# Attention projection of six panels as three f32r products in the last stage, and quantiser scales as bf16 pairs

## The chip, the cores and the metric

The kernel runs on one core of a Trainium2 chip. The core has TensorE (matrix products into PSUM; in the profile PE for the products and PEld for the weight loads that run beside them), VectorE (DVE), ScalarE (ACT), GpSimd (POOL), and SyncE (SP), which issues most of the DMAs. The metric is the device time of one execution in microseconds (us), lower is better.

## What is computed

One layer of a graph network on 1250 nodes with 1024 features and 40000 edges. Cut to what matters here:

```python
xn = layernorm(x)
x = x + gnn(xn, edges) + mix(xn)
x = x + ffn(layernorm(x))

# gnn: attention over incoming edges of each node (4 heads of 64)
p = exp(e - segment_max(e, dst)[dst])
out = segment_sum(p / denom[dst] * xl[src], dst) @ W_up
# mix: linear attention, phi = elu + 1, 16 heads
kv   = einsum('bshd,bshe->bhde', phi(k), v)
attn = einsum('bshd,bhde->bshe', phi(q), kv)
mix  = attn @ Wo + bo
# ffn: every operand is fake-quantised to NVFP4 in blocks of 16
sc8 = e4m3(clip(amax / 6 * global_scale, 0, 448))
q   = sign(x) * nearest_fp4(abs(x) / sc8);  result = q * sc8
```

kv and Wo are multiplied first, into a matrix mix_w of 1024 x 1024. What is left of mix is phi(q) @ mix_w: eight panels of 128 features for each node.

## The kernel before

Nodes come in ten chunks (c = 0 to 9) of 125. `build` runs six stages one after the other; their instructions are ordered by hand, each engine has its own program, and semaphores join them. The change concerns the last two.

**`aggregate`** walks over 81 groups (g) of edges; a group is four pairs (q) of 128 edges. For each group SP loads the edge rows (`load_edges`, line 1649 onwards; the DMA itself is line 92) into one of six slots, once TensorE has finished the group six before. VectorE multiplies the rows of two pairs with their weights (`weigh`, line 1833) and writes the one-hot rows of the four pairs (`one_hot`, line 1839, four slots). ScalarE multiplies the rows of the other two pairs (`scale_rows`, line 1784). GpSimd copies eight further columns into the rows (`extras`, lines 1687 and 1688). TensorE then adds everything up in PSUM (lines 1733 and 1735).

Other work is put between the groups by number:
- The quantiser for the weights of the ffn (`PairQuantiser`): each pair m of weight tiles takes VectorE at g = 6m+1, +3, +4 and +5 (`scaled`, `clip`, `push`, `pull`, `product`, lines 1565 to 1582), ScalarE once, and then TensorE transposes and ScalarE copies (`out_tile`).
- Early panels of phi(q) @ mix_w (`early_projection`, line 1750). `EARLY[c]` says how many of the eight panels of chunk c are done here: 4, 3, 3, 3, 3, 2, 2, 0, 0, 0, in two halves of 512 columns. Each half is a piece: its last product stands at group `ENDS_AT[p]`, ScalarE copies it out of PSUM a group later (`out_piece`, line 1791), GpSimd stores it three groups later (`add_piece`): chunks 0 and 1 by an accumulating DMA into `x_bo` (line 73), the others into DRAM (`part_rows`, line 1698). There is one buffer for pieces; ScalarE's next copy waits until the last piece is stored (`piece_kept`), and TensorE's next piece until the copy is done.

**`finish`** takes chunk after chunk. For chunk c TensorE computes the remaining panels (`mix_part`, line 2081, f32, 8 - EARLY[c] panels in each half) and the gnn part (`gnn_part`, line 2086); this is `projections(c)`. VectorE adds it to x (`residual`, line 2352). ScalarE and VectorE normalise the chunk (`deviation` 2205, `scale_of`, `normalise` 2235), VectorE and ScalarE quantise it (`RowQuantiser`: `scales` 1885 to 1891, `clipped` 1899 and 1900, ScalarE's `size_x` 2214, `rounded` 1911 and 1912, `product` 1917). TensorE transposes it and computes the gates (2132), VectorE forms and quantises the hidden rows with the same lines at 512 columns, TensorE computes the down projection (2145). The three are interleaved: in turn c VectorE does hidden(c-2), residual(c), scale_of(c), clip_h(c-2), clip_x(c), round_h(c-2), round_x(c); TensorE does projections(c), turn_x(c-1), down(c-3), gates(c-1). TensorE may start projections(c) once residual(c-1) is done. Phi for chunk c+2 is loaded by SP into one of two slots of `phi_c` when projections(c) are done (line 2023). `x_bo` gets x, the bias and the early part by three DMAs, the latter two accumulating.

In an f32 product TensorE makes two passes, which the profile shows as two instructions. f32r is a type of 32 bits that takes one. An exact enough product of f32 values is made of three f32r ones: high x high, high x low and low x high, where high is the value as f32r and low what is left. An earlier stage does so already (lines 1064 to 1066).

## Time and profile before

| | us |
|---|---|
| median of 3 runs | 1059.26 |
| lowest and highest | 1058.24, 1063.79 |
| profiled execution, own time | 1058.53 |
| its span in the trace | 1056.8 |

In the profiled execution `aggregate` lasts from about 612 to 816 us and `finish` from there to the end. All times below count from the start of the span. A row of the timeline gives the start, the duration, the engine, the line, the operation with its operands, and in brackets how long the engine was idle before it and what released it. Neighbouring instructions of the same form are merged (x8).

### The profile page before, as it was taken

The numbers are of one execution on the slowest core, as the hardware profiler recorded it, in microseconds if no ns is written. First come the engines' busy times: TensorE is split into PE (matmuls) and PEld (weight loads), VectorE is DVE, ScalarE is ACT, GpSimd is POOL, SyncE is SP. The second block draws the span as 40 slices with busy tenths as digits, with TensorE's granted clock in tenths as the row PEclk, the third lists the DMA queues.
The fourth block names the chain that finished last, engine by engine and source line by source line (L and its number), as shares of the span: only waits on it lengthen the run. The fifth ranks groups of instructions, "written<-read, shape, count | busy, mean of one in ns | idle before, by whom it ended". The sixth has DMA issues, their size and how long they took to land. (4 is left out here: it accounts for less than half of the span.)

```text
span 1056.8 us, 17499 instructions
## 1 busy us (share of the span) xinstructions
PE 959.5 (91%) x5429; PEld 794.3 (75%) x5429; DVE 837.9 (79%) x1395; ACT 648.7 (61%) x1435; POOL 496.7 (47%) x582
## 2 busy tenths in 40 slices
PE   2698879999999999999997779999999879999986
PEld 2676779999999999999997357888898334454443
DVE  5875567888888888888888868998995768887776
ACT  3274446665765766666664568999898335554442
POOL 0211777777777777777771524444444200110000
PEclk9699889999999999999998899999999989999998
DMA  9304588989889898998872689989985364674314
GB/s 246 56 7 110 169 243 259 292 265 280 257 254 294 266 287 284 288 280 282 277 244 91 247 198 332 293 278 310 290 270 192 79 135 122 149 160 112 81 19 79
DMA packets 109977, 221.40 MB, mean 209 GB/s; under 512 B 25883, under 2 KB 58228, under 8 KB 109857
## 3 DMA queue, kind: packets, MB, share of 16 engines
q1 hardware_dynamic: 89053, 159.98, 47.2%
q0 software_dynamic: 20576, 60.08, 23.8%
q8 instruction: 50, 0.82, 0.3%
q10 hardware_dynamic: 260, 0.20, 0.1%
q14 instruction: 38, 0.31, 0.1%
HBM read 156.56 MB, written 62.95 MB: 208 GB/s over the span
## 5 line engine op out<-in xcount | busy, mean ns | idle before, releaser
L1024 POOL DMA_INDIRECT score_gath<-xl_rows,misc x324 | 347.4, 1072 | 101.6 <-issue 92.1
L1064 PE MATMUL score_ps_m<-x_hi,score_w_hi 128*128 128x416 f32 (+1 forms) x576 | 209.4, 363 | 2.1 <-DVE score_w_lo L1217 1.9
L1065 PE MATMUL score_ps_m<-x_lo,score_w_hi 128*128 128x416 f32 (+1 forms) x576 | 204.1, 354 | 0.0
L1066 PE MATMUL score_ps_m<-x_hi,score_w_lo 128*128 128x416 f32 (+1 forms) x576 | 204.1, 354 | 0.0
L1784 ACT ACTIVATE agg_gath<-agg_gath,prob 128x64 f32<-128x64 f32 x648 | 159.2, 353 | 6.7 <-DMA agg_gath<-edge_rows 6.4
L1196 DVE TENSOR_TENSOR score_zb<-score_gath,score_ps_x 128x1024 f32<-128x1024 f32 x81 | 98.8, 1219 | 67.6 <-PE score_ps_x L1047 57.9
L1733 PE MATMUL ps_all<-agg_gath,agg_hot 128*125 128x128 f32 x648 | 128.0, 280 | 9.8 <-DVE agg_hot L1839 6.4
L1735 PE MATMUL ps_all<-agg_gath,agg_hot 128*125 128x136 f32 x648 | 128.9, 281 | 0.0
L1733 PEld LDWEIGHTS ps_all<-agg_gath,agg_hot 128*125 128x125 f32 x648 | 100.5, 189 | 25.8 <-issue 25.2
L2081 PE MATMUL ps_all<-mix_w,phi_c 128*125 128x512 f32 x240 | 108.4, 602 | 5.8 <-DVEq L2355 5.2
L1064 PEld LDWEIGHTS score_ps_m<-x_hi,score_w_hi 128*128 128x128 f32 x576 | 109.7, 190 | 4.2 <-issue 2.6
L1065 PEld LDWEIGHTS score_ps_m<-x_lo,score_w_hi 128*128 128x128 f32 x576 | 110.1, 191 | 1.1
L1066 PEld LDWEIGHTS score_ps_m<-x_hi,score_w_lo 128*128 128x128 f32 x576 | 109.3, 190 | 1.5
L1047 PE MATMUL score_ps_x<-parts,score_mask_t 125*128 x648 | 93.7, 287 | 14.6 <-ACT score_mask_t L1119 14.6
L1047 PEld LDWEIGHTS score_ps_x<-parts,score_mask_t 125*128 125x128 f32 x648 | 90.1, 193 | 17.6 <-issue 17.1
L1203 DVE TENSOR_TENSOR score_zb<-score_zb,misc 128x1024 f32<-128x1024 f32 x81 | 98.8, 1219 | 3.4 <-ACT score_zb L1124 3.4
L1204 DVE TENSOR_REDUCE score_e<-score_zb 128x16 f32<-128x1024 f32 x81 | 98.8, 1220 | 2.8
L1735 PEld LDWEIGHTS ps_all<-agg_gath,agg_hot 128*125 128x125 f32 x648 | 97.2, 190 | 0.0
L1117 ACT ACTIVATE score_mask_t<-local_bc,part_iota 125x512 fp32r<-125x512 bf16 x81 | 58.2, 718 | 56.1 <-DMA local_bc<-local_rows 52.7
L2081 PEld LDWEIGHTS ps_all<-mix_w,phi_c 128*125 128x125 f32 x240 | 45.6, 191 | 62.2 <-issue 55.1
L1124 ACT ACTIVATE score_zb<-score_zb 128x1024 f32<-128x1024 f32 x81 | 85.6, 1057 | 10.4 <-DVE score_zb L1196 10.0
L1687 POOL COPY agg_gath<-prob 128x16 f32<-128x16 f32 x81 | 44.2, 549 | 87.4 <-DMA agg_gath<-edge_rows 74.6
(341 smaller groups left out, 1666.3 us busy)
## 6 DMA issues: line engine op xcount, KB each, us to landing
edge_rows<-score_gath SPq DMA_DIRECT2D x81, 528.0 KB, 3.8
agg_gath<-edge_rows SPq DMA_DIRECT2D x81, 528.0 KB, 5.6
local_bc<-local_rows SPq DMA_DIRECT2D x40, 224.0 KB
score_gath<-xl_rows,misc POOLq DMA_INDIRECT x324, 4.5
phi_c<-phi_rows SPq DMA_DIRECT2D x10, 500.0 KB, 6.1
x_bo<-in_x SPq DMA_DIRECT2D x10, 500.0 KB
x_bo<-in_L_mix_bo POOLq DMA_DIRECT2D x10, 500.0 KB, 7.2
out<-fin_x SPq DMA_DIRECT2D x9, 500.0 KB
```

The costliest lines, as they stand in the source:

```text
L1024: nc.gpsimd.indirect_dma_start(out=gath[:, g % GS, q, :], out_offset=None, in_=xl_rows, in_offset=bass.IndirectOffsetOnAxis(ap=src_idx[:, ...
L1047: m = pe.matmul(ps_x[:, u, q // 2, (q % 2) * HID:(q % 2 + 1) * HID], mask_t[:, u, q * TE:(q + 1) * TE], xr_flat[:, ds(cs[q] * (2 * HID) + ...
L1064: pe.matmul(acc, w_hi[:, i % 2, kk, :], x_hi[:, kk, cols], start=(kk == 0), stop=False)
L1065: pe.matmul(acc, w_hi[:, i % 2, kk, :], x_lo[:, kk, cols], start=False, stop=False)
L1066: mm = pe.matmul(acc, w_lo[:, i % 2, kk, :], x_hi[:, kk, cols], start=False, stop=(kk == KC - 1))
L1196: v.tensor_tensor(zb[:, u, :].rearrange("p (q d) -> p q d", q=GP), gath[:, g % GS, :, 0:HID], ps_x[:, u, :, :].rearrange("p h (q d) -> p ( ...
L1203: own.do(v.tensor_tensor(z, z, att_b[:, :].unsqueeze(1).to_broadcast([P, GP, HID]), ALU.mult))
L1204: own.do(v.tensor_reduce(e16[:, :], zb[:, g % 2, :].rearrange("p (a d) -> p a d", d=DH), AX.X, ALU.add))
L1733: pe.matmul(o_flat[0:C, ds(at[2 * q], HALF)], lhs, gath[:, g % GS, q, 0:HALF], start=False, stop=False, skip_group_check=True)
L1735: m = pe.matmul(o_flat[0:C, ds(at[2 * q + 1], UPPER)], lhs, gath[:, g % GS, q, HALF:XW], start=False, stop=False, skip_group_check=True)
L1784: t = act.activation(part, part, ACT.Copy, scale=k.prob[:, g * GP + q, h:h + 1])
L2081: pe.matmul(ps_y[0:C, half, :], phi_c[:, c % 2, kk, :], mix_w[:, kk, half * 512:half * 512 + 512], start=(kk == EARLY[c]), stop=False)
```

## The change

1. `EARLY` is 2 for all chunks: panels 0 and 1 of every chunk are computed in `aggregate`, which makes 20 pieces of two panels instead of 14 of two to four, a piece every 3.6 groups. The number of early panel products stays at 40, that of late ones at 120. Phi for the early panels comes through a ring of four slots; for chunks 6 to 9 SP waits for a piece before it loads.
2. `mix_part` multiplies panels 2 to 7 as three f32r products each. The high and low parts of mix_w are made by GpSimd in `aggregate` (`split_early`, at groups 8, 18, 28, 38, 48 and 58: a copy and a subtraction of 128 x 1024 each, with a wait between). The low part takes the place of mix_w. Three high parts stay in SBUF; those of panels 5 to 7 are stored to DRAM (`mix_rows`) and loaded back by SP at the start of `finish`, into space that the edge rows held.
3. The high part of phi is a copy by ScalarE (`high_phi`, 128 x 750 a chunk), the low part a subtraction by VectorE (`low_phi`, the same size).
4. Both quantisers write the block scale as two equal bf16 values side by side, and round into bf16 (`pull`, `rounded`), so that the last product (`product`) reads bf16 twice and writes bf16, over blocks of 8 x 2 instead of 16.

```diff
@@ -46,7 +46,9 @@
-EARLY = [4, 3, 3, 3, 3, 2, 2] + [0] * (NC - 7)
+EARLY = [2] * NC
+SPLIT = [2, 3, 4, 5, 6, 7]
+SPLIT_KEPT = 3
@@ -71,6 +73,12 @@
+def split_low(nc, k, n, high):
+    kk = SPLIT[n]
+    nc.gpsimd.tensor_tensor(k.mix_lo[:, kk, :], k.mix_w[:, kk, :], high[:, :].bitcast(F32), ALU.subtract).then_inc(k.s_mix_lo, 1)
@@ -197,6 +207,17 @@
+    gath_bytes = 4 * AGG_SLOTS * GP * XW
+    k.gath_at = nc.sbuf_base - gath_bytes
+    assert 4 * D * (len(SPLIT) - SPLIT_KEPT + 1) <= gath_bytes
+    k.s_mix_lo = ctx.enter_context(nc.semaphore("s_mix_lo"))
+    k.s_mix_hi = ctx.enter_context(nc.semaphore("s_mix_hi"))
+    k.s_mix_kept = ctx.enter_context(nc.semaphore("s_mix_kept"))
+    k.s_mix_back = ctx.enter_context(nc.semaphore("s_mix_back"))
+    k.mix_rows = nc.dram_tensor("mix_rows", (len(SPLIT) - SPLIT_KEPT, P, D), F32, kind="Internal").ap()
+    homes = [k.parts_at, k.parts_at + 4 * D, k.kv_at] + [k.gath_at + 4 * D * n for n in range(len(SPLIT) - SPLIT_KEPT)]
+    k.mix_lo = nc.alloc_sbuf_tensor_at("mix_lo", [P, KC, D], F32R, offset=k.mix_at)
+    k.mix_hi = {kk: nc.alloc_sbuf_tensor_at(f"mix_hi{kk}", [P, D], F32R, offset=at) for kk, at in zip(SPLIT, homes)}
@@ -1551,14 +1583,19 @@
-        t, sc8, inv = self.amax[:, kind, :], self.small[:, 0, :], self.small[:, 1, :]
+        t, inv = self.amax[:, kind, :], self.small[:, 1, :]
+        twos = self.scale_twos().rearrange("p (n t) -> p n t", t=2)
...
-        q.do(v.tensor_tensor(sc8, t, p2, ALU.add))
-        q.do(v.tensor_tensor(sc8, sc8, p2, ALU.subtract))
-        q.do(v.tensor_scalar(t, sc8, 2.0 ** -20, -1.0, ALU.max, ALU.mult))
+        q.do(v.tensor_tensor(inv, t, p2, ALU.add))
+        q.do(v.tensor_tensor(twos, inv.unsqueeze(2).to_broadcast([P, NJ * WB, 2]), p2.unsqueeze(2).to_broadcast([P, NJ * WB, 2]), ALU.subtract))
+        q.do(v.tensor_scalar(t, twos[:, :, 0], 2.0 ** -20, -1.0, ALU.max, ALU.mult))
...
+    def scale_twos(self):
+        return self.small[:, 0, :].bitcast(BF16)
@@ -1575,11 +1612,12 @@
-        self.q.do(self.v.scalar_tensor_tensor(out=self.work, in0=self.coarse, scalar=COARSE, in1=self.work, op0=ALU.max, op1=ALU.subtract))
+        self.q.do(self.v.scalar_tensor_tensor(out=self.coarse, in0=self.coarse, scalar=COARSE, in1=self.work, op0=ALU.max, op1=ALU.subtract))
...
-        return self.v.tensor_tensor(self.blocks(out), self.blocks(self.work), self.wide(0, j), ALU.mult)
+        scale = self.scale_twos()[:, 2 * j * self.nb:2 * (j + 1) * self.nb]
+        return self.v.tensor_tensor(by_twos(out), by_twos(self.coarse), twos_over_blocks(scale, self.nb), ALU.mult)
@@ -1647,6 +1686,9 @@
+                def load_early_phi(c):
+                    sp.dma_start(phi_o[:, c % 4, :, :], k.phi_rows[0:2, :, C * c:C * c + C].rearrange("k p n -> p k n")).then_inc(s_phi_o[c % 4], 16)
@@ -1666,8 +1708,12 @@
-                        for c in range(2, 7):
-                            sp.dma_start(phi_o[:, c - 2, :, :], k.phi_rows[0:3, :, C * c:C * c + C].rearrange("k p n -> p k n")).then_inc(s_phi_o, 16)
+                        for c in range(2, 6):
+                            load_early_phi(c)
+                    for c in range(6, NC):
+                        if g == ENDS_AT[2 * (c - 4) + 1] + 4:
+                            sp.wait_ge(s_piece, 2 * (c - 4) + 2)
+                            load_early_phi(c)
@@ -1697,8 +1743,22 @@
+                def split_early(n):
+                    kk = SPLIT[n]
+                    if n > SPLIT_KEPT:
+                        pool.wait_ge(k.s_mix_kept, 16 * (n - SPLIT_KEPT))
+                    high = k.mix_hi[kk] if n < SPLIT_KEPT else mix_stage
+                    nc.gpsimd.tensor_copy(high[:, :], k.mix_w[:, kk, :]).then_inc(k.s_mix_hi, 1)
+                    pool.wait_ge(k.s_mix_hi, n + 1)
+                    split_low(nc, k, n, high)
+                    if n >= SPLIT_KEPT:
+                        nc.gpsimd.dma_start(k.mix_rows[n - SPLIT_KEPT, :, :], mix_stage[:, :].bitcast(F32)).then_inc(k.s_mix_kept, 16)
...
+                    for n in range(len(SPLIT)):
+                        if g == 8 + 10 * n:
+                            split_early(n)
@@ -1880,15 +1940,20 @@
-        t, sc8, inv = (self.small[0:C, i, 0:nb] for i in (0, 2, 3))
+        t, inv = (self.small[0:C, i, 0:nb] for i in (0, 3))
+        twos = self.scale_twos(nb).rearrange("p (n t) -> p n t", t=2)
...
-        q.do(v.tensor_tensor(sc8, t, p2, ALU.add))
-        q.do(v.tensor_tensor(sc8, sc8, p2, ALU.subtract))
-        q.do(v.tensor_scalar(t, sc8, 2.0 ** -20, -1.0, ALU.max, ALU.mult))
+        q.do(v.tensor_tensor(inv, t, p2, ALU.add))
+        q.do(v.tensor_tensor(twos, inv.unsqueeze(2).to_broadcast([C, nb, 2]), p2.unsqueeze(2).to_broadcast([C, nb, 2]), ALU.subtract))
+        q.do(v.tensor_scalar(t, twos[:, :, 0], 2.0 ** -20, -1.0, ALU.max, ALU.mult))
...
+    def scale_twos(self, nb):
+        return self.small[0:C, 2, :].bitcast(BF16)[:, 0:2 * nb]
@@ -1909,14 +1974,12 @@
-        q.do(v.scalar_tensor_tensor(out=a, in0=b, scalar=COARSE, in1=a, op0=ALU.max, op1=ALU.subtract))
+        q.do(v.scalar_tensor_tensor(out=b, in0=b, scalar=COARSE, in1=a, op0=ALU.max, op1=ALU.subtract))
...
-        return self.v.tensor_tensor(out.rearrange("p (n s) -> p n s", s=16),
-                                    self.work[0:C, 0:width].rearrange("p (n s) -> p n s", s=16),
-                                    self.small[0:C, 2, 0:nb].unsqueeze(2).to_broadcast([C, nb, 16]), ALU.mult)
+        return self.v.tensor_tensor(by_twos(out), by_twos(self.coarse[0:C, 0:width]), twos_over_blocks(self.scale_twos(nb), nb), ALU.mult)
@@ -2016,6 +2083,9 @@
+                for n in range(SPLIT_KEPT, len(SPLIT)):
+                    sp.wait_ge(k.s_mix_kept, 16 * (len(SPLIT) - SPLIT_KEPT))
+                    sp.dma_start(k.mix_hi[SPLIT[n]][:, :].bitcast(F32), k.mix_rows[n - SPLIT_KEPT, :, :]).then_inc(k.s_mix_back, 16)
@@ -2077,9 +2147,18 @@
+                    cols = slice(half * 512, half * 512 + 512)
+                    if half == 0:
+                        pe.wait_ge(s_phi_lo, c + 1)
...
-                        pe.matmul(ps_y[0:C, half, :], phi_c[:, c % 2, kk, :], mix_w[:, kk, half * 512:half * 512 + 512],
-                                  start=(kk == EARLY[c]), stop=False)
+                        if half == 0:
+                            pe.wait_ge(k.s_mix_lo, SPLIT.index(kk) + 1)
+                            if kk in SPLIT[SPLIT_KEPT:]:
+                                pe.wait_ge(k.s_mix_back, 16 * (len(SPLIT) - SPLIT_KEPT))
+                        high, low = phi_hi[:, c % 2, kk, :], phi_lo[:, c % 2, kk, :]
+                        pe.matmul(ps_y[0:C, half, :], high, k.mix_hi[kk][:, cols], start=(kk == EARLY[c]), stop=False)
+                        pe.matmul(ps_y[0:C, half, :], high, k.mix_lo[:, kk, cols], start=False, stop=False)
+                        pe.matmul(ps_y[0:C, half, :], low, k.mix_hi[kk][:, cols], start=False, stop=False)
@@ -2090,9 +2169,8 @@
-                    pe.wait_ge(s_phi[c % 2], 16 * (c // 2 + 1))
+                    mix_part(c, 0)
...
-                    mix_part(c, 0)
@@ -2240,6 +2317,12 @@
+                def high_phi(c):
+                    act.wait_ge(s_phi[c % 2], 16 * (c // 2 + 1))
+                    act.activation(phi_hi[:, c % 2, EARLY[c]:, :], phi_c[:, c % 2, EARLY[c]:, :], ACT.Copy).then_inc(s_phi_hi, 1)
+                high_phi(0)
+                high_phi(1)
@@ -2300,7 +2387,16 @@
+                def low_phi(c):
+                    part = phi_c[:, c % 2, EARLY[c]:, :]
+                    v.wait_ge(s_phi_hi, c + 1)
+                    v.tensor_tensor(phi_lo[:, c % 2, EARLY[c]:, :], part, phi_hi[:, c % 2, EARLY[c]:, :].bitcast(F32),
+                                    ALU.subtract).then_inc(s_phi_lo, 1)
+                low_phi(0)
...
+                low_phi(1)
@@ -2424,6 +2522,8 @@
                     round_h(c - 2)
+                    if c + 2 < NC:
+                        low_phi(c + 2)
                     round_x(c)
```

How the instructions stand before and after, at three places. Line numbers of the changed kernel are its own: 1733 and 1734 are `extras`, 1751 and 81 the split, 75 the accumulating DMA.

GpSimd in `aggregate`, around group 8, before:

```order
L1688 COPY agg_gath<-run_max 128x4x4
L73 DMA x_bo<-agg_piece 125x512
L1687 COPY agg_gath<-prob 128x4x4
L1688 COPY agg_gath<-run_max 128x4x4
L1687 COPY agg_gath<-prob 128x4x4
```

The same place now:

```order
L1734 COPY agg_gath<-run_max 128x4x4
L1751 CAST mix_hi_12248<-mix_w 128x1024
L81 TENSOR_TENSOR mix_lo<-mix_w,mix_hi_12248 128x1024
L75 DMA x_bo<-agg_piece 125x512
L1733 COPY agg_gath<-prob 128x4x4
```

Before, the row of the DMA is that of piece 0, behind group 6. Now piece 0's stands behind group 5, and what is shown is the end of group 8 with the first split and piece 1's add behind it.

VectorE in `finish`, the end of the turn of chunk 7 (L1917 and L1982 are the quantiser's last product; `fin_hq` is the hidden row, `misc` holds the quantised x), before:

```order
L1912 SCALAR_TENSOR_TENSOR prob<-prob 125x512
L1917 TENSOR_TENSOR fin_hq<-prob,fin_hid_small 125x512
L1911 SCALAR_TENSOR_TENSOR score<-parts,score 125x1024
L1912 SCALAR_TENSOR_TENSOR score<-parts,score 125x1024
L1917 TENSOR_TENSOR misc<-score,fin_small 125x1024
```

Now:

```order
L1977 SCALAR_TENSOR_TENSOR prob<-prob 125x512
L1982 TENSOR_TENSOR fin_hq<-prob,fin_hid_small 125x512
L2394 TENSOR_TENSOR fin_phi_lo<-phi_c,fin_phi_hi 128x750
L1976 SCALAR_TENSOR_TENSOR score<-parts,score 125x1024
L1977 SCALAR_TENSOR_TENSOR parts<-parts,score 125x1024
L1982 TENSOR_TENSOR misc<-parts,fin_small 125x1024
```

The subtraction for the chunk after next stands between the quantising of the hidden row and that of x.

TensorE at the start of `finish` (L2076 are the transposes of the gnn rows), before:

```order
L1735 MATMUL ps_all<-agg_gath,agg_hot 125x136
L1641 UNCONDITIONAL_BRANCH
L2069 UNCONDITIONAL_BRANCH
L2081 MATMUL ps_all<-mix_w,phi_c 125x512 x8
L2076 MATMUL ps_all<-ident,prob 128x125 x4
```

Now, where the numbers behind mix_hi name the buffers of the panels, 12248 for panel 2:

```order
L1795 MATMUL ps_all<-agg_gath,agg_hot 125x136
L1680 UNCONDITIONAL_BRANCH
L2139 UNCONDITIONAL_BRANCH
L2159 MATMUL ps_all<-mix_hi_12248,fin_phi_hi 125x512
L2160 MATMUL ps_all<-mix_lo,fin_phi_hi 125x512
L2161 MATMUL ps_all<-mix_hi_12248,fin_phi_lo 125x512
L2159 MATMUL ps_all<-mix_hi_12249,fin_phi_hi 125x512
```

Eight f32 products of chunk 0 have become 36 f32r ones, for panels 2 to 7 in two halves, and those of panels 5 to 7 wait for SP's loads.

## Rows read from the trace of the kernel before

**Rows 1.** Busy time by stretch: length, then busy us of each engine, clock, DMA share, GB/s.

```profile
640.00:766.00 126.00, 122.39 (x931) 106.32 (x930) 116.90 (x159) 120.80 (x462) 59.68 (x116) 1.00 0.93 302
766.00:816.00 50.00, 49.17 (x402) 45.27 (x400) 38.65 (x54) 48.11 (x186) 23.92 (x43) 1.00 0.75 245
```

**Rows 2.** Waits of VectorE and of ScalarE, 640 to 766 us: total, times, longest.

```profile
DVE agg_gath L1833 <- DMA agg_gath<-edge_rows: 4.1, 5, 1.4
...
ACT agg_coarse L1806 <- DVEq L1855: 4.0, 2, 2.8
```

**Rows 3.** Timeline of VectorE, line 2352, chunks 0, 1, 2, 4, 8 and 9.

```profile
828.07 1.22 DVE L2352 SCALAR_TENSOR_TENSOR fin_x<-x_bo,ps_all 125x1024 f32<-125x1024 f32 x1 [0.57 <-PE ps_all L2086]
847.69 1.22 DVE L2352 SCALAR_TENSOR_TENSOR fin_x<-x_bo,ps_all 125x1024 f32<-125x1024 f32 x1 [0.22 <-DVE misc L1917]
870.86 1.22 DVE L2352 SCALAR_TENSOR_TENSOR fin_x<-x_bo,ps_all 125x1024 f32<-125x1024 f32 x1 [0.22 <-DVE fin_hid L2386]
908.57 1.22 DVE L2352 SCALAR_TENSOR_TENSOR fin_x<-x_bo,ps_all 125x1024 f32<-125x1024 f32 x1 [0.25 <-DVE fin_hid L2386]
993.07 1.22 DVE L2352 SCALAR_TENSOR_TENSOR fin_x<-x_bo,ps_all 125x1024 f32<-125x1024 f32 x1 [4.45 <-PE ps_all L2086]
1016.13 1.22 DVE L2352 SCALAR_TENSOR_TENSOR fin_x<-x_bo,ps_all 125x1024 f32<-125x1024 f32 x1 [4.45 <-PE ps_all L2086]
```

**Rows 4.** TensorE: from the chain of waits (bf16, f32), then from the timeline (f32r).

```profile
929.43 3.45 PE ps_all L2132 x16
...
952.52 6.87 PE ps_all L2081 x16
...
162.09 0.35 PE L1064 MATMUL score_ps_m<-x_hi,score_w_hi 128*128 128x418 f32 x1
...
163.61 0.35 PE L1066 MATMUL score_ps_m<-x_hi,score_w_lo 128*128 128x418 f32 x1
```

**Rows 5.** VectorE's instructions by form in `finish`: total, mean ns | idle before.

```profile
L1899 DVE TENSOR_TENSOR score<-kv,fin_small 125x1024 f32<-125x1024 f32 x9 | 11.0, 1224 | 0.3
...
L1899 DVE TENSOR_TENSOR prob<-fin_hid,fin_hid_small 125x512 f32<-125x512 f32 x10 | 6.9, 692 | 1.2
...
L1906 DVE TENSOR_SCALAR prob<-prob 125x512 int16<-125x512 int16 x2 | 0.7, 346 | 0.1
```

**Rows 6.** TensorE in `finish`: the chain, the timeline, and the stretch behind 849 us.

```profile
816.25 7.10 PE ps_all L2081 x16
...
849.04 6.61 PE L2081 MATMUL ps_all<-mix_w,phi_c 128*125 128x512 f32 x10 [4.98 <-DVEq L2355]
...
849.00:853.00 4.00, 3.96 (x5) 1.81 (x6) 2.81 (x12) 1.54 (x3) 0.00 (x0) 0.50 0.55 143
```

**Rows 7.** DMA issues, 585 to 600 and 625 to 680 us: size, median us to landing.

```profile
max_wo<-in_L_mix_Wo SPq DMA_DIRECT2D x4, 512.0 KB, 4.4
...
x_bo<-agg_piece POOLq DMA_DIRECT2D x4, 250.0 KB, 7.1
```

**Rows 8.** GpSimd's instructions by form over the whole trace.

```profile
L501 POOL TENSOR_TENSOR parts<-xr,parts 125x256 fp32r<-125x256 f32 x10 | 7.3, 734 | 47.9 <-ACT parts L651 47.9
...
L463 POOL MEMSET kv<- 128x1024 f32 x1 | 0.9, 942 | 0.0
```

**Rows 9.** Timeline of GpSimd and VectorE in an early stage.

```profile
60.08 0.73 POOL L501 TENSOR_TENSOR parts<-xr,parts 125x256 fp32r<-125x256 f32 x1 [10.53 <-ACT parts L651]
60.15 0.94 DVE L780 SCALAR_TENSOR_TENSOR zsum<-zsum 125x256 f32<-125x256 f32 x1
...
71.22 0.42 DVE L780 SCALAR_TENSOR_TENSOR zsum<-zsum 125x256 f32<-125x256 f32 x1
```

**Rows 10.** Timeline of GpSimd: piece 0's add, and the last of `extras` of group 8.

```profile
632.43 0.83 POOL L73 DMA_DIRECT2D x_bo<-agg_piece  x1 [1.07 <-DMA x_bo<-in_L_mix_bo]
...
639.51 0.66 POOL L1688 COPY agg_gath<-run_max 128x16 f32<-128x16 f32 x1
```

More of the change, by code:

```diff
@@ L1536, with by_twos, twos_over_blocks @@
 COARSE = NEAR_ONE * 2.0 ** 22
+def by_twos(ap):
+    return ap.rearrange("p (n r t) -> p n r t", r=8, t=2)
+def twos_over_blocks(row, nb):
+    return row.rearrange("p (n t) -> p n t", t=2).unsqueeze(2).to_broadcast([row.shape[0], nb, 8, 2])
 class PairQuantiser:
@@ L1620, in aggregate @@
         ps_w = ps_m[:, 1, 0:256].bitcast(BF16).rearrange("p (b f) -> p b f", f=P)
-        phi_of = lambda c: k.phi_c[:, c, :, :] if c < 2 else phi_o[:, c - 2, :, :]
+        phi_of = lambda c: k.phi_c[:, c, :, :] if c < 2 else phi_o[:, c % 4, :, :]
         s_load = k.s_load
@@ L1628, in aggregate @@
         s_agg = sem("s_agg")
-        s_phi_o = sem("s_phi_o")
+        s_phi_o = [sem(f"s_phi_o{i}") for i in range(4)]
         s_step = sem("s_step")
@@ L1996, in finish @@
         s_tail = sem("s_tail")
+        s_phi_hi = sem("s_phi_hi")
+        s_phi_lo = sem("s_phi_lo")
         s_pself = sem("s_pself")
@@ L2411, in _ @@
                 clip_x(0)
+                low_phi(2)
                 round_x(0)
@@ L2417, in _ @@
                 clip_x(1)
+                low_phi(3)
                 round_x(1)
```

21 lines of the change are left out of this document (15 added, 6 removed).

## Prediction

> **What bounds the kernel now.** I read the busy time by stretch first, then the waits of each engine there, then the timeline of the places that the change touches. The page names no engine as the bound of the whole, so each of the two stages touched is read by itself.
>
> The aggregation stage ends at 816 us. In its stretch 640 to 766 us three engines are full at once: TensorE 122.4, ScalarE 120.8 and VectorE 116.9 of 126 us [rows 1]. What VectorE lacks is mostly the gap of some 0.06 us between dependent instructions; it really waits 4.1 us there, and ScalarE 4.0 [rows 2]. So some 4 to 5 us of additional work on VectorE finds room, and what is over that moves the stage. From 766 us on VectorE has 11 us free, ScalarE under 2 [rows 1].
>
> The last stage handles ten chunks of 125 nodes. The start of line 2352 marks each: 828.07, 847.69, 870.86, two later 908.57, and 993.07 and 1016.13 for the last two [rows 3]. From 870.86 to 908.57 the period is 18.86 us, and VectorE itself releases the next. The period of the last is 23.07 us, and VectorE waits 4.45 us in it for TensorE. So the early chunks are bound by VectorE and the late ones, which have eight late panels instead of five, by TensorE. Behind 1016.13 the chain is nearly all VectorE's.
>
> **TensorE's products.** An f32 product of 128x512 is two instructions of 0.43 us (16 in 6.87), 0.859 in all. An f32r product is one. Its pace at 512 columns isn't in the trace: at 418 columns it is 0.190 us (162.09 to 163.61 for 8) [rows 4], which by columns gives 0.233. The lower bound is bf16's pace at 512, 0.216 (16 in 3.45); 0.25 is my upper one. Three cost 0.70 instead of 0.86. There are 120 late panels before and after, only spread evenly (12 products of a chunk instead of 8 to 16), and 40 early ones. What else is in a period is 23.07 - 16 x 0.859 = 9.3, so TensorE's period becomes 9.3 + 12 x 0.70 = 17.7 us. That is less than VectorE's: TensorE stops being the bound, and its gain is capped there.
>
> **VectorE in the last stage.** Each chunk adds one subtraction of 128x750 (low_phi): between 512 elements at 0.692 and 1024 at 1.224 [rows 5] that is 0.94, and 0.03 of gap. The quantiser's last product now reads bf16 and bf16, and no row shows such a one. Bounds for 1024 elements: 1.22, as before, and 0.69, twice the pace; half of that for 512. I take the lower ones, because line 1906, with 16 bits in and out, does 512 elements in 0.346, twice 0.692's pace [rows 5]. The Trainium skill ("VectorE: DVE Perf Modes", the perf-mode tier table) has tensor_tensor in bf16 at two elements a cycle, so by it the sum stays. Saved: 0.53 + 0.27 = 0.80. Scales written twice (64 more elements, then 32) add 0.10. Period: 18.86 + 0.97 - 0.80 + 0.10 = 19.13 us. ScalarE gets a copy of 750 elements a chunk, 0.9 us at about 1.15 ns each; it lies before a wait for VectorE, and low_phi covers a late one.
>
> **The start of the last stage.** Before, TensorE starts its panels at 816.25 and ends them at 823.35 [rows 6]; residual 0 follows 4.7 us later. Now ScalarE copies phi, VectorE ends its node steps and subtracts (to 819.0), and TensorE starts 3 us late. Panels 5 to 7 wait for three loads of 512 KB that SP issues only at 816.3. Such a load lands 4.4 us after its issue [rows 7]; two more behind it take 1.7 each at the 300 GB/s of [rows 1]: all landed at 824. 27 products follow, 6.3 us. TensorE has then stood twice for some 3 us. Behind a wait of 4.98 us at 849.04 its granted clock was 0.50, the lower level (1.2 GHz), for 4 us [rows 6]; I add 2 us for that. Panels end at 832.4: +9.0.
>
> Chunk by chunk: residual 0 at 837.1. Residual 1 (VectorE's interval, 19.62 + 0.97 - 0.53 + 0.13): 857.3. Residual 2 (TensorE's interval, 23.17, less 0.5 of panels): 880.0. Six periods of 19.13: residual 8 at 994.8. The last period has no low_phi, 18.2: residual 9 at 1013.0 instead of 1016.13: -3.1. The tail holds one product of 1024 and three of 512: -1.34, scales +0.13. The last stage yields **-4.3 us** (bounds +2 and -9: loads landed at 829 or 821, clock cost 4 or 0, ends of the product's pace).
>
> **The aggregation stage.** TensorE's work there is unchanged, VectorE saves 12 x 0.53. GpSimd gets six splits at groups 8, 18, ... 58, each a copy and a subtraction of 128x1024. GpSimd's rows: a memset of 128x1024 takes 0.94, a subtraction of 125x256 into f32r 0.73, times four 2.9 [rows 8]. I take 1.1 for the copy, which is nearest to the memset, and 2.7 for the subtraction, since a part of the 0.73 is fixed: 3.8 a split, bounds 3.3 and 5.2.
>
> This isn't free for VectorE. At 60.08 GpSimd subtracts for 0.73 us; VectorE's line 780 starts at 60.15 and takes 0.94, to 0.28 us behind GpSimd's end. The same instruction alone takes 0.42, at 71.22 [rows 9]. So GpSimd's instruction locked VectorE's out for its whole length, all but 0.14 us of start. The Trainium skill ("SBUF — State Buffer", Who interferes with whom) states this: a VectorE instruction with two SBUF inputs and a GpSimd one that reads SBUF exclude each other for the whole instruction. The trace agrees, and the rule speaks against this change; all of VectorE's large instructions in the stage are of that kind or rival it for the same ports.
>
> VectorE loses 6 x (3.8 - 2 x 0.14) = 21 us between groups 8 and 60. It saves 9 x 0.53 = 4.8 there and pays 0.5 for longer scales. Of the net 16.8 its waits take 4.1 to 5. It may run up to four groups ahead of TensorE, so I take 1 more off: **+11**.
>
> Two waits more. Pieces come every 3.6 groups instead of 5.1, and one may overwrite the last only when the add of that has landed, 7.1 us after its issue [rows 7]. Piece 0's add goes out at 632.4 and so lands at 639.5; ScalarE now wants piece 1 at group 6, some 3 us sooner. Piece 1's add stands behind the first split on GpSimd: group 8's extras end at 640.2 [rows 10], the split near 645, the add lands at 652.5, while ScalarE wants to overwrite it at group 10, near 650. Behind both stand the weighted rows that TensorE needs. Of these 3 + 2.5 us the first split's lock hides 3.5: **+2**. Six piece copies more on ScalarE (0.6 each) lie mostly in the stretch that VectorE then binds. SP's four waits for a piece delay one edge load each by 2 to 3 us, within the lead of six slots. The stage: **+13** (bounds +5 and +20).
>
> **Sum.** 1058.5 (the profiled execution's own time; the median of the runs is 0.7 more) + 13 - 4.3 = **1067 us**.
>
> **Rivals.**
> 1. *The lock is absorbed.* If GpSimd's split holds VectorE only where it has time, or runs at twice my pace, VectorE's savings and waits pay for it. It decides below 9 us of lock in all, 1.5 a split. Against it: the exclusion at 60.08 [rows 9] is complete, and VectorE has hardly a gap. For it: four slots of one-hot rows and six of edge rows let it run ahead. Then only ScalarE's 3.6 us are left, half hidden: 1058.5 + 1.8 - 4.3 = 1056, not slower than before.
> 2. *The adds hold ScalarE throughout.* 7.1 us of landing stand against 8.9 us from piece to piece, and splits at groups 48 and 58 delay an add again, with 3 MB more to move in a stage whose DMA engines are 93% busy [rows 1]. It decides when an add lands over 8 us behind its copy. At 3 us each for two or three more pieces: 1075.
> 3. *bf16 pairs run at the old pace,* since the innermost run is two elements and nothing here shows such a shape. Last stage 0.8 x 8 + 1.3 = 7.7 more, aggregation 4.8 more: 1079.
> 4. *TensorE's clock falls in each chunk,* since it now waits some 1.4 us in a period. 4 us at the lower level cost 2, of which the slack takes 1.4; over six chunks at most 4 more: 1071.
>
> **Chances.** Forecast 0.52 (1060 to 1075), rival 1 0.20, rival 2 0.12, rival 3 0.06, rival 4 0.05, other 0.05. A difference of 0.5% (5.3 us) is about what a measurement of this kernel tells from none: faster is below 1054, slower above 1064.6. Rival 1 puts half of its chance below 1054, the forecast 0.20 of its own under 1064.6. Faster 0.13, same 0.33, slower 0.54. The range of 1054 to 1077 leaves out rival 3, the upper end of rival 2 and the lower end of rival 1.
>
> **What would show it.** In the aggregation stage: six places where VectorE's instructions of 0.7 us take over 2 while line 81 runs on GpSimd; 10 us or more of waits of TensorE for VectorE or ScalarE; its last group near 829 instead of 816. A product into the bf16 tile at 0.69. In the last stage: f32r products 0.233 apart, the first residual 21 us behind the stage's start instead of 12, periods of 19.1, no waits of 4.45. The forecast is wrong if the aggregation keeps its length, or if the mix_hi loads land before TensorE needs them.

## The result: 1.5% slower

The changed kernel takes 1074.65 us (median of 4 runs, 1073.58 to 1075.28), the kernel before, on the same chip, 1058.75 (1057.07 to 1063.79). The ratio is 1.0146, with a 95% interval of 1.0119 to 1.0172. The forecast had the direction and its range held the time, but it said +8 us and the change costs +16. The profiled executions have spans of 1056.8 and 1073.3 us; what follows is worked out against these.

**Where the time went.** The first and the last product of the aggregation stage mark its length. Two rows of the product line of each kernel, before and then after (instruction, count, shortest/median/longest in ns, first and last start in us):

```profile
L1733 PE MATMUL ps_all<-agg_gath,agg_hot x648: 272/273/542, 612.7 to 815.2; 128*125 128x128 f32 x162
```

```profile
L1793 PE MATMUL ps_all<-agg_gath,agg_hot x648: 272/273/573, 611.6 to 838.6; 128*125 128x128 f32 x162
```

With the end of the very last product (815.8 and 839.2) the stage is 203.0 us long before and 227.5 after: **+24.5**. The last stage, from there to the end, falls from 241.1 to 234.2: **-6.9**. The stage also starts 1.0 us earlier, which is no effect of the change: over all kernels below, none of which changes the work ahead of it, it starts between 610.5 and 616.2. +24.5 - 6.9 - 1.0 = +16.6; the spans differ by 16.5.

The busy times of the aggregation stage as a whole, first of before and then of after (columns: window, its length, then busy us and instructions of TensorE, its weight loads, VectorE, ScalarE, GpSimd; granted clock; DMA share; GB/s):

```profile
612.70:815.80 203.10, 194.09 (x1472) 170.19 (x1472) 174.85 (x238) 184.44 (x705) 90.13 (x170) 0.99 0.89 280
```

```profile
611.70:839.30 227.60, 201.74 (x1472) 177.05 (x1472) 185.68 (x238) 187.32 (x711) 110.56 (x191) 0.96 0.82 264
```

TensorE executes the same 1472 instructions. It is busy 7.7 us longer, at a mean granted clock of 0.96 instead of 0.99, and idle 25.9 us instead of 9.0: the +24.5 are **16.8 us more of waiting and 7.7 us of lower clock**. The forecast had no term for the second. Whom it waits for, and what ScalarE waits for (engine, line, what ended the wait: us in all, times, longest), 612 to 840 us:

```profile
PE ps_all L1793 <- DVE agg_hot L1899: 10.1, 6, 3.1
PE ps_all L1793 <- POOL agg_gath L1734: 6.6, 3, 4.1
PE ps_all L1793 <- ACT agg_gath L1844: 4.9, 2, 3.5
PE ps_all L1793 <- POOL agg_gath L1733: 2.6, 2, 2.1
...
ACT agg_piece L1851 <- DMA part_rows<-agg_piece: 10.5, 3, 8.0
ACT agg_piece L1851 <- DMA x_bo<-agg_piece: 9.0, 1, 9.0
```

Before, no piece copy of ScalarE waited for a DMA at all. Now four of the 20 do, for 19.5 us together.

**The split.** The first of the two lines of GpSimd is the copy, the second the subtraction:

```profile
L1751 POOL CAST mix_hi<-mix_w x3: 1035/1037/1497, 638.1 to 690.6; 128x1024 fp32r<-128x1024 f32 x3
L81 POOL TENSOR_TENSOR mix_lo<-mix_w,mix_hi x3: 2656/2662/2686, 639.2 to 691.7; 128x1024 fp32r<-128x1024 f32 x3
```

1.04 + 2.66 = 3.7 us each; the forecast had 3.8. VectorE's two instructions beside the split at group 48, by the timeline, GpSimd first:

```profile
752.83 1.04 POOL L1751 CAST agg_mix_stage<-mix_w 128x1024 fp32r<-128x1024 f32 x1
753.96 2.66 POOL L81 TENSOR_TENSOR mix_lo<-mix_w,agg_mix_stage 128x1024 fp32r<-128x1024 f32 x1
...
757.13 0.54 POOL L1744 DMA_DIRECT2D part_rows<-agg_piece  x1
```

```profile
752.84 1.57 DVE L1893 TENSOR_TENSOR agg_gath<-agg_gath,prob 128x512 f32<-128x512 f32 x1
754.33 2.82 DVE L1899 TENSOR_TENSOR agg_hot<-node_iota,dst_local 128x500 f32<-128x500 f32 x1
```

Alone they take 0.69 and 0.67. The first ends 0.5 us behind the copy, the second 0.5 behind the subtraction: 3.0 us are lost. (The Trainium skill's rule in "SBUF — State Buffer", Who interferes with whom, that a VectorE instruction with two SBUF inputs and a GpSimd one that reads SBUF shut each other out for a whole instruction, holds here once more.) An instruction of VectorE with one input was held too: its line 1607, 0.69 us alone, took 1.57 at 638.06, beside the copy of the first split at 638.05. The row at 757.13 is the store of a piece that ScalarE had copied at 748.81: it stood behind the split. ScalarE's next rows:

```profile
748.81 0.58 ACT L1851 ACTIVATE agg_piece<-ps_all 125x512 f32<-125x512 f32 x1
...
753.18 3.92 ACT L1844 ACTIVATE agg_gath<-agg_gath,prob 128x64 f32<-128x64 f32 x16
765.08 0.60 ACT L1851 ACTIVATE agg_piece<-ps_all 125x512 f32<-125x512 f32 x1 [7.98 <-DMA part_rows<-agg_piece]
```

**The clock.** At 639.0 ScalarE ends its wait of 9.0 us, for the landing of the first piece. TensorE's wait of 3.48 us for the rows that ScalarE weights ends at 641.65. The window around and behind that, which answers to [rows 1]:

```profile
641.00:647.00 6.00, 5.35 (x24) 5.36 (x25) 5.71 (x8) 6.00 (x24) 4.71 (x10) 0.50 0.88 256
```

TensorE's granted clock is 0.50, the lower level (1.2 GHz): busy for 5.35 us, it gets 24 instructions done; the kernel before does 42 in 5.59 us of the same window. The same comes again at 696 and at 764 us, behind waits of 4.06 us for GpSimd and 3.03 us for VectorE.

**The last stage.** The residuals, which answer to [rows 3], are now line 2448:

```profile
L2448 DVE SCALAR_TENSOR_TENSOR fin_x<-x_bo,ps_all x10: 1220/1220/1222, 857.3 to 1033.0; 125x1024 f32<-125x1024 f32 x10
```

They start at 857.30, 876.86, 900.02, 919.39, 938.41 and so on to 1014.82 and 1033.0. The start of the stage:

```profile
839.58 1.28 SPq L2088 DMA_DIRECT2D mix_hi<-mix_rows  x3
...
842.49 0.79 PE L2159 MATMUL ps_all<-mix_hi,fin_phi_hi 128*125 128x512 f32 x1 [3.40 <-DVE fin_phi_lo L2394]
843.08 0.63 PE L2160 MATMUL ps_all<-mix_lo,fin_phi_hi 128*125 128x512 f32 x1
...
846.34 0.39 PE L2160 MATMUL ps_all<-mix_lo,fin_phi_hi 128*125 128x512 f32 x1
846.57 0.39 PE L2161 MATMUL ps_all<-mix_hi,fin_phi_lo 128*125 128x512 f32 x1
```

The last two are 0.23 us apart: that is the pace of an f32r product. No product waits for the three loads.

### The profile page after: what moved, and what is told of

Read it like the earlier page. It is cut to its first block and busy times, and to the rows that moved or that the text cites. A ratio compares the mean times of both kernels' runs of the same rounds, so it can differ in the third digit from the quotient of the medians.

```text
span 1073.3 us, 17839 instructions
## 1 busy us (share of the span) xinstructions
PE 949.0 (88%) x5549; PEld 822.9 (77%) x5549; DVE 850.3 (79%) x1405; ACT 658.4 (61%) x1451; POOL 518.0 (48%) x606
## 5 line engine op out<-in xcount | busy, mean ns | idle before, releaser
L1793 PE MATMUL ps_all<-agg_gath,agg_hot 128*125 128x128 f32 x648 | 132.3, 287 | 26.5 <-DVE agg_hot L1899 11.0
L1793 PEld LDWEIGHTS ps_all<-agg_gath,agg_hot 128*125 128x125 f32 x648 | 104.1, 196 | 41.2 <-issue 40.9
L1795 PE MATMUL ps_all<-agg_gath,agg_hot 128*125 128x136 f32 x648 | 133.1, 288 | 0.0
L1795 PEld LDWEIGHTS ps_all<-agg_gath,agg_hot 128*125 128x125 f32 x648 | 101.2, 197 | 0.0
L1893 DVE TENSOR_TENSOR agg_gath<-agg_gath,prob 128x512 f32<-128x512 f32 x81 | 63.2, 780 | 20.4 <-DMA agg_gath<-edge_rows 15.8
L1733 POOL COPY agg_gath<-prob 128x16 f32<-128x16 f32 x81 | 40.0, 498 | 73.1 <-DMA agg_gath<-edge_rows 62.6
L2159 PE MATMUL ps_all<-mix_hi,fin_phi_hi 128*125 128x512 f32 x120 | 54.3, 453 | 8.8 <-DVEq L2451 5.4
```

Source lines behind the costliest of these rows:

```text
L1793: pe.matmul(o_flat[0:C, ds(at[2 * q], HALF)], lhs, gath[:, g % GS, q, 0:HALF], start=False, stop=False, skip_group_check=True)
L1795: m = pe.matmul(o_flat[0:C, ds(at[2 * q + 1], UPPER)], lhs, gath[:, g % GS, q, HALF:XW], start=False, stop=False, skip_group_check=True)
```

## The experiments

All ratios are to the kernel before on the same chip, with 95% intervals; the medians move with the chip, so the ratios are what to compare. The first look at the traces left two causes for the additional 24 us: the splits on GpSimd, and the single piece tile, which ScalarE may overwrite only when the last piece has landed. It could be both or one alone.

The stage lengths are from one profiled execution of each. The kernel before alone takes from 1054 to 1065 us in its executions, so a difference of two stage lengths can be off by some us, and two ratios differ surely only by more than some 0.3 to 0.4% (3 to 4 us). `nosplit` and `nosplit_two` leave out the low half of the weights: they show a price and are no kernels to use.

| kernel | ratio | interval | aggregation | rest |
|---|---|---|---|---|
| before | 1 | | 203.0 | 241.1 |
| changed | 1.0146 | 1.0119 to 1.0172 | 227.5 | 234.2 |
| nosplit | 1.0043 | 1.0016 to 1.0070 | 215.6 | 233.9 |
| two_pieces | 1.0109 | 1.0079 to 1.0138 | 221.5 | 233.9 |
| nosplit_two | 0.9964 | 0.9939 to 0.9989 | 209.6 | 233.1 |
| even_pairs | 1.0044 | 1.0023 to 1.0066 | 213.6 | 237.9 |
| even_pairs_two | 1.0007 | 0.9986 to 1.0028 | 206.2 | 237.8 |
| pairs | 0.9946 | 0.9921 to 0.9971 | 202.3 | 238.2 |
| splits_only | 1.0136 | 1.0081 to 1.0190 | 218.1 | 241.9 |
| vhold | 1.0185 | 1.0163 to 1.0208 | 220.4 | 241.4 |
| adds_first | 1.0167 | 1.0148 to 1.0187 | 224.7 | 231.9 |
| halves_two | 1.0045 | 1.0018 to 1.0072 | 218.6 | 233.6 |
| light_two | 1.0002 | 0.9975 to 1.0029 | 214.1 | 233.2 |

**nosplit: the changed kernel without splits.**

```
-                    nc.gpsimd.tensor_copy(high[:, :], k.mix_w[:, kk, :]).then_inc(k.s_mix_hi, 1)
-                    pool.wait_ge(k.s_mix_hi, n + 1)
-                    split_low(nc, k, n, high)
+                    pool.sem_inc(k.s_mix_lo, 1)
...
-                        pe.matmul(ps_y[0:C, half, :], high, k.mix_hi[kk][:, cols], start=(kk == EARLY[c]), stop=False)
+                        pe.matmul(ps_y[0:C, half, :], high, mix_high(kk)[:, cols], start=(kk == EARLY[c]), stop=False)
```

> The changed kernel without its six splits on GpSimd: mix_w's panels 2 to 7 are stored once and serve as both halves, so the low half of the weights is wrong; the panels' stores and loads and all twelve late f32r products stay. Theory: the aggregation stage's +24.5 us is two causes together, GpSimd's splits (which shut VectorE out and push the piece stores back) and the one piece tile that ScalarE must find free. Of the waits of ScalarE for a piece the first (9.0 us) stands ahead of the first split and stays, the one of 8.0 us goes: the stage is 5 to 8 us longer than before instead of 24.5, the last stage keeps its -7: 1058. Rival A, the splits alone: stage as before, 1050 to 1052. Rival B, the pieces alone: 1068 to 1072.

Measured: ratio 1.0043, 1063.85 us, with the stage 12.6 us longer than before; 6 us over the theory, which had the stage 5 to 8 longer, and 4 under rival B. The splits are 11.9 us of the stage, and 1.03% or 11 us by the ratios. ScalarE's waits of this kernel, same window:

```profile
ACT agg_piece L1849 <- DMA x_bo<-agg_piece: 8.8, 1, 8.8
...
ACT agg_piece L1849 <- DMA part_rows<-agg_piece: 4.7, 2, 3.3
```

The long wait of 8.0 us is gone, the first one stands. The splits are not the only cause, since the stage is still 12.6 us longer than before; the pieces are not the only one either, since the stage got 11.9 shorter without the splits.

**two_pieces: the changed kernel with two piece tiles in turn** (the second one in a free part of `parts`, and one store semaphore for each; ScalarE now also waits for the last stores at the start of the last stage, which is no longer for it).

```
-                        piece_kept(act, k, p - 1, PIECES)
-                    act.activation(piece[:, :], ps_y, ACT.Copy).then_inc(s_piece, 1)
+                        piece_kept(act, k, p - 2, PIECES)
+                    act.activation(piece[p % 2][:, :], ps_y, ACT.Copy).then_inc(s_piece, 1)
```

> The changed kernel with two piece tiles in turn, so that ScalarE waits for the piece before the last. Theory: the lock stays, about 13 us in the stage, and ScalarE's 19.5 us of waits for a piece's landing go: 1063 to 1066. Rival A (splits alone): 1073 to 1075, no gain. Rival B (pieces alone): 1052 to 1056.

Measured: ratio 1.0109, 1071.87 us. No piece copy waits for a DMA any more, and the stage is 6.0 us shorter. The gain is 4 us by the ratios, where I expected some 10: the theory is off in size. The intervals overlap, so the times alone do not rule out rival A, no gain; the waits that are gone speak against it, and so do the two pairs of runs below. Of the 19.5 us that ScalarE waited, two thirds or more were hidden behind other waits. TensorE now waits more for VectorE, 13.6 us instead of 10.1:

```profile
PE ps_all L1793 <- DVE agg_hot L1899: 13.6, 8, 4.2
PE ps_all L1793 <- POOL agg_gath L1733: 4.2, 1, 4.2
```

**nosplit_two: both together.**

> The changed kernel without splits (as in the run without splits, the low half of the weights is wrong) and with two piece tiles. Theory: what is left of the stage's extra 12.6 us there is the wait for the piece's landing; with two tiles it falls to about 4 (six more piece copies of 0.6 us on ScalarE), the total to 1054 to 1057. Rival: the crowding of loads and the stores of 3 MB cost it, not the piece tile: 1060 to 1064. If splits and pieces add up, the difference to the run with two tiles and splits is the lock alone, 11 to 16 us.

Measured: ratio 0.9964, 1055.97 us, as the theory had it, the stage 209.6 us. By stage length the two causes add up: taking the splits out gives 11.9 us with one tile (227.5 to 215.6) and 11.9 with two (221.5 to 209.6); the second tile gives 6.0 with splits and 6.0 without. So close an agreement of single executions is luck. By the ratios the splits are worth 1.03% (11 us) with one tile and 1.45% (15 us) with two, and the second tile 0.37% (4 us) with splits and 0.79% (8 us) without, each to within some 0.4%. Both causes are clear of noise; whether one hides a part of the other isn't settled. 6.6 us more than before are left.

**even_pairs and even_pairs_two: the change without f32r.** Panels 0 and 1 of all chunks early and the bf16 pairs, with f32 products and no splits, first with one piece tile, then with two.

```
-EARLY = [4, 3, 3, 3, 3, 2, 2] + [0] * (NC - 7)
+EARLY = [2] * NC
...
-        phi_o = sb("phi_o", [P, 5, 3, C])
+        phi_o = sb("phi_o", [P, 4, 2, C])
```

> The change without f32r products: panels 0 and 1 of all chunks early, bf16 pairs, and f32 products for panels 2 to 7, no splits at all. Theory: TensorE's period in the last stage is 9.3 + 12 x 0.859 = 19.6 us against 19.1 in the changed kernel, but the stage starts 5 to 6 us sooner, and the aggregation stage is 5 to 8 us longer than before by the waits for pieces: 1056 to 1060. Rival: the f32r products are what makes the last stage shorter; without them it isn't, 1064 to 1067.

> Panels 0 and 1 of all chunks early, bf16 pairs, f32 products in the last stage, no splits, two piece tiles. Theory: 6 to 8 us of the aggregation stage's extra 10.6 go, 1056 to 1058. Rival: the waits for the first piece were hidden behind the load of edge rows that ends at the same time, 1062 to 1065.

Measured: 1.0044 and 1.0007, or 1064.13 and 1058.15 us. The first is 4 us over the theory and within the rival's range, but not for the rival's reason: the last stage did get 3.2 us shorter without f32r. It is the even distribution of the early panels that makes the aggregation stage 10.6 us longer; the second piece tile takes 7.4 of them back (4 us by the ratios), and the total is within 0.2 us of the theory's range. The last stage is 237.9 us, against 233.9 to 234.2 with f32r products. So the f32r products are worth some 4 us, and the splits that they need cost 11 to 12 in the stage before.

**pairs: the kernel before with bf16 pairs only.**

```
-        self.q.do(self.v.scalar_tensor_tensor(out=self.work, in0=self.coarse, scalar=COARSE, in1=self.work, op0=ALU.max, op1=ALU.subtract))
+        self.q.do(self.v.scalar_tensor_tensor(out=self.coarse, in0=self.coarse, scalar=COARSE, in1=self.work, op0=ALU.max, op1=ALU.subtract))
...
-        return self.v.tensor_tensor(self.blocks(out), self.blocks(self.work), self.wide(0, j), ALU.mult)
+        return self.v.tensor_tensor(by_twos(out), by_twos(self.coarse), twos_over_blocks(scale, self.nb), ALU.mult)
```

> The kernel before with the quantiser scales as bf16 pairs and nothing else of the change. Theory: the product into the bf16 tile takes half of the time, VectorE gains 0.5 us a product in the aggregation stage, where it is hardly waited for (0 to -1), and 0.8 us in each period of the last stage that VectorE binds (three or four) and 1.3 in the tail: 1053 to 1056. Rival: the late chunks are TensorE's and the rest is absorbed, 1057 to 1059.

Measured: 1054.54 us, ratio 0.9946, as the theory had it. The stage is unchanged (202.3), the last one 2.9 us shorter. This is **the lowest ratio of all, clear of both kernels**; of `nosplit_two`, 0.9964, it is not told apart.

**splits_only: the kernel before with the six splits and nothing else.**

```
+                def split_dump(n):
+                    nc.gpsimd.tensor_copy(dump[0][:, :], k.mix_w[:, 2 + n, :]).then_inc(s_dump, 1)
+                    pool.wait_ge(s_dump, 2 * n + 1)
+                    nc.gpsimd.tensor_tensor(dump[1][:, :], k.mix_w[:, 2 + n, :], dump[0][:, :].bitcast(F32), ALU.subtract).then_inc(s_dump, 1)
```

> The kernel before with the six splits on GpSimd at groups 8, 18, ... 58 and nothing else of the change: copy and subtraction go into two unused tiles, no store, no load, nobody waits for them. Theory: the splits alone make the stage some 11 us longer (21 us of lock less the room of VectorE), 1068 to 1072, with VectorE's instructions beside a subtraction at 2 us and more; the pieces come every 5 groups here, so a store that the split pushes back should still cost ScalarE nothing. Rival: without the crowded pieces the lock finds room in the lead of VectorE, 1059 to 1063.

Measured: ratio 1.0136, 1073.37 us: a little over the theory, far over the rival. The profiled execution took 1076.63 us, 3 more than the median. VectorE, whose instructions are those of before, is busy 16.9 us longer:

```profile
614.80:833.00 218.20, 200.91 (x1472) 174.34 (x1472) 191.73 (x238) 185.31 (x705) 114.96 (x182) 0.96 0.83 260
```

```profile
PE ps_all L1743 <- DVE agg_hot L1849: 16.7, 14, 3.8
```

16.9 / 6 = 2.8 us a split. No piece copy of ScalarE waits for a landing here: pieces five groups apart leave the single tile time enough even behind a split. TensorE's +15.1 us are 8.3 of waiting and 6.8 of lower clock.

**vhold: the kernel before with VectorE itself held.**

```
+                    if g in range(8, 60, 10):
+                        for i in range(3):
+                            own.do(v.tensor_tensor(dump[:, :], k.mix_w[:, 2, :], k.mix_w[:, 3, :], ALU.subtract))
```

> The kernel before with three additional subtractions of 128x1024 (1.2 us each, into an unused tile) on VectorE itself at groups 8, 18, ... 58, and no splits: VectorE is held for 3.7 us where a split would shut it out, while GpSimd stays free. Theory: a split costs what it takes of VectorE's time, so this costs the same as the splits alone did, 1069 to 1074, and TensorE waits for the one-hot rows of VectorE. Rival: what counts is GpSimd's own delay (its small copies and its stores come later), or its traffic; then this is clearly cheaper, 1058 to 1064.

Measured: ratio 1.0185, 1075.84 us, over the theory's range and far from the rival's. It costs somewhat more than the splits, and takes more of VectorE:

```profile
610.80:831.30 220.50, 199.82 (x1472) 174.45 (x1472) 196.65 (x256) 185.22 (x705) 92.31 (x170) 0.97 0.84 258
```

VectorE is busy 21.8 us longer (196.65 instead of 174.85), 3.6 us a place. GpSimd has the same 170 instructions as before, so VectorE's time is enough to explain the price of the splits: 1.85% for 21.8 us here, 1.36% for 16.9 there. That GpSimd's own delay adds nothing isn't shown by it.

**adds_first: the changed kernel with piece stores ahead of the split in groups 8 and 48.**

```
-                    for n in range(len(SPLIT)):
-                        if g == 8 + 10 * n:
-                            split_early(n)
...
                         if g == ENDS_AT[p] + 3:
                             add_piece(p)
+                    for n in range(len(SPLIT)):
+                        if g == 8 + 10 * n:
+                            split_early(n)
```

> The changed kernel with one thing moved: in a group where both stand, GpSimd issues the piece's add or store ahead of the split. That concerns groups 8 and 48. Theory: ScalarE's wait of 8.0 us for the store issued behind the split of group 48 falls by the split's 3.7 us, the one at group 8 was hidden by other waits: 1069 to 1073. Rival: the 8.0 us were hidden behind the lock anyway, 1074 to 1076.

Measured: ratio 1.0167, 1074.08 us: no gain, the rival is right. The trace shows the edit working and not helping:

```profile
ACT agg_piece L1851 <- DMA x_bo<-agg_piece: 8.1, 1, 8.1
...
ACT agg_piece L1851 <- DMA part_rows<-agg_piece: 6.8, 3, 2.4
```

The wait of 8.0 us is now 2.4 at most, and the time is the same. ScalarE's copy now comes at 761.5, but TensorE's wait of 4.53 us, which ends at 764.5, is for VectorE's one-hot rows. So most of the single tile's price is elsewhere; what stands in every kernel with one tile and 20 pieces (9.0, 8.8, 8.9 and 8.1 us) is the first wait, which ends between 639 and 643 us. That this one wait is the whole price was not tried by itself.

**halves_two and light_two: the same splits in halves, and then in other places.** Both have two piece tiles and twelve halves of 512 columns; the first at groups 8, 13, ... 63, the second at 8, 14, ... 74.

```
-                        if g == 8 + 10 * n:
-                            split_early(n)
+                        if g == 8 + 6 * n:
+                            split_early(n // 2, n % 2)
```

> The changed kernel with two piece tiles and each split cut in two halves of 512 columns, one at every fifth group (8, 13, ... 63). The lock's sum stays at 22 us, but each is 1.9 us long. Theory: VectorE runs one to four groups ahead, so a lock of 1.9 us reaches TensorE seldom: 4 to 8 us less than with whole splits, 1063 to 1068. Rival: VectorE has no time to win a lead back between them, the sum counts and not the length: 1070 to 1073.

> As the run with halved splits and two piece tiles, with the twelve halves at groups 8, 14, 20, ... 74, which are groups in which VectorE has no part of the quantiser, and three of them behind 766 us, where it has time. Theory: VectorE has 1.2 to 1.9 us less to do in such a group and wins its lead back, 2 to 4 us less than at every fifth group: 1059 to 1062. Rival: the lead evens this out and only the sum counts: 1063 to 1065.

Measured: 1.0045 (1064.17 us) and 1.0002 (1059.09 us), against 1.0109 for whole splits. A half subtraction takes 1.59 us, so the sum of the splits is no smaller (VectorE is busy 184.0 and 184.5 us, 186.6 with whole ones). Cut in two, they cost 0.64% or 7 us less; in groups without quantiser work another 0.43%. Both are as the theories had them, so the sum of the splits doesn't set the price alone; length and place count. The place is two things here: light_two avoids the quantiser's groups, and it also puts three halves behind 766 us, where VectorE has time [rows 1]. Which of the two counts wasn't tried apart. The aggregation stage of halves_two, and that of light_two, where TensorE's busy time is that of the kernel before, 194.1, and its clock 0.98:

```profile
613.20:832.00 218.80, 200.21 (x1472) 176.40 (x1472) 184.02 (x238) 187.96 (x711) 116.67 (x203) 0.95 0.85 274
```

```profile
610.80:825.00 214.20, 194.12 (x1472) 170.63 (x1472) 184.48 (x238) 187.90 (x711) 120.89 (x203) 0.98 0.87 280
```

Against nosplit_two, its bound from below, the splits still cost 0.38% (4 us, hardly clear of noise), instead of the 1.45% of whole ones at every tenth group.

## Why the prediction was right in its sign and short in its size

**The lock: right.** The forecast had 21 us of lock and +11 net. Measured: 2.8 to 3.0 us a split instead of 3.5, some 17 in all, and the stage lost 11.9 (changed kernel) to 15.1 (kernel before). vhold shows that the loss of so much of VectorE's time is enough for it. But the route to the sum was off in two places that cancel: VectorE's lead hid more than I allowed (TensorE waits only 8.3 us more in splits_only), and the lower clock behind these waits, for which the working had no term in this stage, cost 6.8 us that this lead had saved.

**The two waits for a piece: the step that failed.** I wrote +2 for a sum of 3 + 2.5 us of waits less what the first split hides. The tile costs 6.0 by stage length, 4 to 8 by the ratios. Of the two places only the first was right, the piece of group 6. At the second, the copy of group 10 at 649.29, ScalarE waited for no landing: the first split was over at 641.8 and not near 645, and the add behind it went out at 641.78. The two copies:

```profile
639.02 0.60 ACT L1851 ACTIVATE agg_piece<-ps_all 125x512 f32<-125x512 f32 x1 [9.00 <-DMA x_bo<-agg_piece]
...
649.29 0.60 ACT L1851 ACTIVATE agg_piece<-ps_all 125x512 f32<-125x512 f32 x1 [0.56 <-PE ps_all L1810]
```

The long wait behind a split came at group 48 instead, and cost nothing that adds_first could win back. At the first place the size was wrong. I set piece 0's add at 632.4 with a landing at 639.5, and charged "some 3 us sooner". The landing was at 639.0, as forecast, but ScalarE stood from 630.0 on, since it had done group 6 while TensorE was at group 4. TensorE's products for the piece end at 631.8, so 7 us of the wait are the landing's alone, where I had 3 from the order. TensorE then waited 3.48 us and ran 24 instructions at half pace. What I took for 3 us, half hidden, was a wait of 7 with a tail. Whether "the first split's lock hides 3.5" is open: by stage length the tile costs 6.0 with splits and without, by the ratios 4 with and 8 without, which is not resolved.

**"Six piece copies more lie mostly in the stretch that VectorE then binds": wrong too.** The sum had nothing for them. With no split and no wait for a landing, the stage is still 3.2 us (even_pairs_two) to 6.6 us (nosplit_two) longer than before; by the ratios even_pairs_two costs 0.6% more than pairs, which differs by the early panels and the second tile. Six copies of 0.6 us on an engine that was 96% busy [rows 1] are 3.6. What the other 3 are in nosplit_two, which also stores 1.5 MB from GpSimd's queue, wasn't tried apart; both figures are of one execution each.

**Rival 2 had a part of it.** It said 1075, which is the time, by adds that hold ScalarE throughout. They hold it four times, 19.5 us, but two_pieces shows that only some 4 to 6 of these count. That its time matched is luck: the measured sum is another one, splits 11.9, tile 6.0 and the rest, copies and stores, 6.6.

**The start of the last stage: right wait, wrong load.** Residual 0 stands 18.2 us behind the end of the stage before instead of 12.4, +5.9 where I had +9.0. Of this 3.4 us are the six late panels instead of four, which even_pairs shows alone (15.8). TensorE's late start of 3.4 us and the half pace behind it came as forecast. The loads didn't: issued from 839.6 on, none was waited for when TensorE came to panel 5 at 846.1, its tenth product. I had 7.7 us from the first issue to the last landing and 27 products behind that; it was at most 6.5, and TensorE's own late start covered it. By the prediction's own last sign this part of the forecast failed: the loads landed before TensorE needed them.

**The periods: right.** 19.56, 23.16, then 19.0 to 19.4 and 18.2 us, for 20.2, 22.7, 19.13 and 18.2. The terms, each by its row:

```profile
L2394 DVE TENSOR_TENSOR fin_phi_lo<-phi_c,fin_phi_hi x10: 934/941/943, 841.5 to 1009.5; 128x750 fp32r<-128x750 f32 x10
L1982 DVE TENSOR_TENSOR misc<-parts,fin_small x10: 691/691/693, 876.0 to 1049.3; 125x1024 bf16<-125x1024 bf16 x10
L1982 DVE TENSOR_TENSOR fin_hq<-prob,fin_hid_small x10: 424/425/425, 913.5 to 1065.8; 125x512 bf16<-125x512 bf16 x10
```

The bf16 product of 1024 is at 0.691 as taken; that of 512 is 0.425, which is the saving of 0.27 that the sum had. Together they save (1.224 - 0.691) + (0.691 - 0.425) = 0.80. From the first residual to the last it is 175.7 us, where the forecast had 175.9.

**The tail: given back.** 40.3 us instead of 40.7; I had -1.2. VectorE did its part up to there 1.0 us faster and then waited for TensorE, whose 16 bf16 products took 5.49 us, against 3.67 at this place in the kernel before:

```profile
1053.55 5.49 PE L2210 MATMUL ps_all<-gate_q,misc 128*125 128x512 bf16 x16 [1.26 <-ACT misc L2272]
1059.16 0.75 DVE L2482 SCALAR_TENSOR_TENSOR fin_hid<-ps_all,fs,fin_e 125x512 f32<-125x512 f32 x1 [1.88 <-PE ps_all L2210]
```

In nosplit, two_pieces and pairs, where these 16 products took 3.62 to 3.67 us, the tail is 38.8 to 39.0 us.

Of the other rivals, the first (the lock is absorbed) falls with splits_only; the third (pairs at the old pace) by the rows above; the fourth (clock falling in each chunk) by a granted clock of 1.00 in each of the six periods from 900.0 to 1014.8 us. One of them:

```profile
938.50:957.50 19.00, 17.81 (x82) 11.86 (x81) 16.80 (x36) 11.11 (x15) 2.13 (x3) 1.00 0.70 164
```

TensorE was to need 17.7 us of such a period, and is busy for 17.81.

What the sum missed in the aggregation stage, in the prediction's terms: 11.9 for the splits where it had +11 net of what VectorE saves, 6.0 for the two waits where it had +2, and 6.6 where it had nothing; +24.5 instead of +13, outside its bounds of +5 to +20. The last stage gave 6.9 instead of 4.3. So the range held the time partly by luck.

## What to carry to other kernels

Ahead of an engine that is full, cost a new wait from where the waiting engine stands in time, not from the order of the program, and expect TensorE to lose clock behind it: between nothing and nearly as much again as the wait, in these runs. A buffer used more often needs the landing of its transfer counted in periods: 14 pieces left a single tile free every time, 20 did not. GpSimd work that shuts out VectorE costs by the length of a piece and by its place more than by its sum: in halves, at other groups, the same splits cost about a quarter. And take a bundle apart: one of the three edits here was a gain by itself.
